# First feed-forward layer on tokens sorted by expert in DRAM, with the whole first attention ahead of it

## What is computed

```
x = x + _L0_xattn_ref(_layernorm(x), ctx, ...)        # one head, 32 keys per sequence
x = x + _L0_ffn_ref(_layernorm(x), ...)               # 8 experts, each token uses ONE (argmax of the gates)
x = x + _L1_xattn_ref(_layernorm(x), ctx, ctx, ...)   # 16 heads, 32 keys
x = x + _L1_ffn_ref(_layernorm(x), ...)               # 16 experts, top 4 per token, and a shared expert
```

## Time and profile before

| | |
|---|---|
| time, median of 3 runs | 404.8 us (399.02 and 426.97 the others) |
| the profiled execution | span 400.2 us from the first to the last instruction; that page gives no time beside it |
| TensorE, VectorE, ScalarE, GpSimd busy | 355.2, 252.4, 189.4, 165.3 us |
| chain that ended last | TensorE 62%, VectorE 22%, issue 9% |
| DMA | 8.14 MB, mean 20 GB/s |

### The profile page before, as it was taken

One profiled execution on the slowest core, in us unless ns is written; L12 is line 12 of the kernel. 1 busy time (PEld: TensorE's weight loads), 2 busy tenths in 40 slices (PEclk: granted clock), 3 DMA queues, 4 the chain that ended last, 5 costly groups with the idle time before them and its releaser, 6 DMA issues.

```text
span 400.2 us, 5681 instructions
## 1 busy us (share of the span) xinstructions
PE 355.2 (89%) x1871; PEld 276.1 (69%) x1875; DVE 252.4 (63%) x608; ACT 189.4 (47%) x316; POOL 165.3 (41%) x161
## 2 busy tenths in 40 slices
PE   0885999999999999999889967797849999999995
PEld 0673778877787788777466756574528878878883
DVE  4445526644564454863799999979974665665652
ACT  1525524662546364545455533474424445444452
POOL 5539302100210151432385631736743555555553
PEclk9988699999999999999999998999978999999998
DMA  7604000000000000000000000000000000000000
GB/s 264 247 1 162 7 2 1 2 0 2 1 1 2 2 0 2 1 2 1 0 2 1 2 0 0 2 1 1 0 0 2 27 2 0 26 0 0 26 0 26
DMA packets 2408, 8.14 MB, mean 20 GB/s; under 512 B 432, under 2 KB 544, under 8 KB 2000
## 3 DMA queue, kind: packets, MB, share of 16 engines
q1 hardware_dynamic: 1984, 6.49, 4.4%
q10 hardware_dynamic: 400, 1.34, 1.0%
HBM read 6.78 MB, written 1.05 MB: 20 GB/s over the span
## 4 chain that ended last, share of the span: by engine, by line
PE 62%; DVE 22%; issue 9%; ACT 2%; DMA 2%; POOL 1%; POOLq 0%; another core or an unknown queue 0%; SPq 0%; ACTq 0%; DVEq 0%
PE bank L1112 58%; DVE xn L808 3%; DVE sc L944 3%; DVE mx L937 2%; PE bank L1124 2%; DMA pack_a<-in_pack_a 2%; DVE act L1073 1%; DVE z L949 1%; DVE st L797 1%; PE bank L1299 1%; DVE bqrep L878 1%; DVE rz L953 1%; PE bank L1163 1%; DVE route L972 1%; POOL an L738 1%
## 5 line engine op out<-in xcount | busy, mean ns | idle before, releaser
L759 POOL TENSOR_TENSOR w1l<-hm,w1h 128x512 fp32r<-128x512 f32 x48 | 62.2, 1298 | 41.8 <-ACT w1h L604 41.6
L913 DVE TENSOR_TENSOR hm<-act,bank 128x512 f32<-128x512 f32 x64 | 43.3, 685 | 52.3 <-ACT act L520 51.6
L1112 PEld LDWEIGHTS bank<-w,hm 128*128 128x128 f32 x512 | 65.6, 195 | 10.1 <-issue 5.1
L1112 PE MATMUL bank<-w,hm 128*128 128x128 f32 x512 | 71.8, 286 | 0.1
L520 ACT ACTIVATE act<-bank,pack_b 128x512 f32<-128x512 f32 x64 | 43.4, 687 | 56.6 <-PE bank L1112 55.9
L1073 DVE TENSOR_TENSOR act<-act,bank 128x512 f32<-128x512 f32 x48 | 33.0, 687 | 38.9 <-ACT act L619 38.7
L619 ACT ACTIVATE act<-bank 128x512 f32<-128x512 f32 x48 | 28.7, 598 | 51.8 <-PE bank L1112 51.5
L663 POOL TENSOR_SCALAR ve<-mv 128x4 f32<-128x4 f32 x16 | 3.7, 228 | 113.0 <-DVE mv L801 109.0
L1112 PE MATMUL bank<-xTh,gu1h 128*128 (+3 forms) x104 | 43.5, 418 | 2.4 <-DVE act L1073 2.4
L1112 PE MATMUL bank<-xTh,gu1l 128*128 (+3 forms) x104 | 41.8, 402 | 0.0
L1112 PE MATMUL bank<-xTl,gu1h 128*128 (+3 forms) x104 | 41.6, 400 | 0.0
(11 more groups left out here) (198 smaller groups left out, 671.5 us busy)
## 6 DMA issues: line engine op xcount, KB each, us to landing
wf<-in_gu SPq DMA_DIRECT2D x1, 1632.0 KB, 7.2
x<-in_x SPq DMA_DIRECT2D x4, 256.0 KB, 9.3
wf<-in_w ACTq DMA_DIRECT2D x1, 1024.0 KB, 6.6
w<-in_w SPq DMA_DIRECT2D x1, 1024.0 KB, 11.4
out_x<-x SPq DMA_DIRECT2D x4, 256.0 KB, 2.0
w<-in_w SPq DMA_DIRECT2D x1, 768.0 KB, 12.7
pack_a<-in_pack_a SPq DMA_DIRECT2D x1, 455.0 KB, 6.0
pack_b<-in_pack_b SPq DMA_DIRECT2D x1, 360.0 KB, 8.4
```

What stands on the lines that cost most here:

```text
L759: nc.gpsimd.tensor_tensor(hml_slot(r)[0:m], hm_slot(r)[0:m], hmh_slot(r)[0:m].bitcast(F32), ALU.subtract).then_inc(s.hml_ready, 1)
L913: nc.vector.tensor_tensor(hm[:, r % 4, :], act[:, r % 4, :], bank[2 + r // 2 % 2][:, :], ALU.mult).then_inc(s.hm_ready, 1)
L1112: return nc.tensor.matmul(dst, lhsT, rhs, start=start, stop=stop, skip_group_check=True)
```

## The change

The first feed-forward layer is computed for one expert per token. The items and `AFTER` are gone, and so is `experts0`. In their place, in order of time:

1. **First attention ahead.** `STEPS0` has 14 steps; in step s chunk c does stage k = s - 2c, of `STAGES0` = 8 (0 statistics; 1 norm, transposes, scores; 2 shift and exp; 3 softmax and output; 4 residual and statistics; 5 norm and logits; 6 one-hot; 7 slot). `normalise` is on ScalarE now, as `x * rstd + shift_of`; `rstd_of` has two small instructions more on GpSimd.
2. **Slots and tables.** Matmuls with a triangle and with ones count the tokens of the same expert ahead of each token; `slot0` is expert x REGION + rank. GpSimd writes each normalised tile of 128 rows to its slots in DRAM (`scatter`, 16 indirect DMAs, in stage 7 of each chunk). About 12 VectorE instructions on one partition (`over0` to `tile_r`) work out, for each of T0 = 16 + 8 - 1 = 23 row tiles, its expert and its first row. SyncE reads them into registers, and writes zero rows behind the last token of each expert (9 DMAs).
3. **23 row tiles.** SyncE loads, per tile, the expert's weights `wb` (128x642, 321 KB) and the rows `xs` (128x128, 64 KB) into SLOTS0 = 4 buffers. TensorE transposes the rows, multiplies by W1, and one tile later by W2, all plain FP32; VectorE copies the transpose and adds b2, ScalarE does Gelu; GpSimd stores each result to DRAM (23 DMAs).
4. **Back.** When all are stored, GpSimd fetches each tile of 128 tokens with an indirect DMA (`fetch`, 16; 8 ahead of the second attention, 8 in its steps), and VectorE adds `score * y` to `x` (`combine`).
5. **Second attention.** As before, but all four chunks' query norms stand in or just ahead of it. The rounding of its neighbour's weights is ahead of or among the row tiles: high halves on ScalarE, low halves on VectorE.

`experts1` is unchanged except that `normalise` is on ScalarE.

```diff
-AFTER = {XT: 0, SCORES: 1, EXP0: 2, SOFTMAX: 3, ATTN_T: 5, OUT: 6, NORM2: 7, XT2: 9, LOGITS: 10, EXP0G: 11, GATES: 12,
-         GATES_T: 14, BIAS2: 15, STATS: 14, NORM: 15}
+STAGES0, LAG0 = 8, 2
+STEPS0 = [[(s - LAG0 * c, c) for c in range(B) if 0 <= s - LAG0 * c < STAGES0] for s in range(STAGES0 + LAG0 * (B - 1))]
...
+            for t in range(0, T0, SLOTS0):
...
+                for u in own:
+                    if u >= SLOTS0:
+                        sp.wait_ge(s.y0_ready, u - SLOTS0 + 1)
+                    load_weights(u, experts[u - t])
+                    if u == 0:
+                        sp.wait_ge(s.scattered, 16 * NT)
+                        sp.wait_ge(s.padded, 16 * (E0 + 1))
+                    load_tokens(u, first[u - t])
...
+            for t in range(T0):
+                pool.wait_ge(s.y0_ready, t + 1)
+                pool.dma_start(ys_dram[t * P:(t + 1) * P, :], ys[:, t % SLOTS0, :]).then_inc(s.kept_y[t % SLOTS0], 16)
+            pool.wait_ge(s.home_ready, 1)
+            for i in range(SLOTS0):
+                pool.wait_ge(s.kept_y[i], 16 * len(range(i, T0, SLOTS0)))
+            for t in range(2 * TPB):
+                fetch(t)
+            rstd_of(2, 0)
...
+            for t in range(T0 + 2):
+                if t < T0:
+                    pe.wait_ge(s.ld_xs[t % SLOTS0], rounds0(t))
...
+                    nc.tensor.transpose(bank[t % 2][:, 0:P], xs[:, t % SLOTS0, :], ident).then_inc(s.xs_mm, 1)
+                if 1 <= t <= T0:
+                    u = t - 1
+                    pe.wait_ge(s.ld_wb[u % SLOTS0], rounds0(u))
+                    pe.wait_ge(s.xsT_ready, u + 1)
...
+                        last = mm(bank[2 + u % 2][:, k * P:(k + 1) * P], w0_1[:, u % SLOTS0, k, :], xsT[:, u % 2, :])
...
+                if t >= 2:
+                    u = t - 2
+                    pe.wait_ge(s.h0_ready, u + 1)
...
+                        last = mm(bank[4 + u % 2][:, 0:C], hT0[:, u % 2, k, :], w0_2[:, u % SLOTS0, k, :],
+                                  start=(k == 0), stop=(k == HID0 - 1))
```

More of the change, by code:

```diff
@@ L14 @@
 F32R = mybir.dt.float32r
+I32 = mybir.dt.int32
 BF16 = mybir.dt.bfloat16
@@ new lines, in _, with round_gu, round_w2 @@
+            keys_values(3)
+            def round_gu(n):
+                w, q = divmod(n, 4)
+                width = (R1 * P + I1) // 4
+                nc.scalar.copy(gu1h[:, w, q * width:(q + 1) * width], gu1f[:, w, q * width:(q + 1) * width]).then_inc(s.guh_ready, 1)
+            def round_w2(n):
+                src, rows, own = w2_piece(n)
+                nc.scalar.copy(w2h[rows, own, :], src).then_inc(s.w2h_ready, 1)
+            act_e.wait_ge(s.ld_gu, 16)
+            for n in range(PIECES):
+                round_gu(n)
@@ L739, in _ @@
                                             ALU.mult).then_inc(s.an1_ready, 1)
-                if i == LN3:
-                    rstd_of(2, B - 1)
+                for b in ahead(i, FETCH3):
+                    rstd_of(2, b)
+                if i + 2 * TPB < NT:
+                    fetch(i + 2 * TPB)
                 for b in starts(i, ADD):
@@ new lines, in _ @@
+            v.wait_ge(s.ld_b, 16)
+            step(nc.vector.tensor_scalar(bo16[:, :], bo1, 1.0 / H1, None, ALU.mult))
+            v.wait_ge(s.kv_ready, 4)
+            for b in range(B):
+                block_diagonal(vT1, Vblk, b, s.vblk_ready)
+            v.wait_ge(s.move_mm, 1)
+            step(nc.vector.tensor_tensor(rk0[:, :, :, :].rearrange("p b j e -> p (b j) e"), rows_of(bank[0][:, 0:E0], NT), oh16[:, :, :], ALU.mult))
+            step(nc.vector.tensor_reduce(z0[:, :, :].rearrange("p b j -> p (b j)"), rk0[:, :, :, :].rearrange("p b j e -> p (b j) e"), AX, ALU.add))
@@ L934, in maxima, with combine @@
+            def combine(b):
+                v.wait_ge(s.fetched[b], 16 * TPB)
+                for t in range(b * TPB, (b + 1) * TPB):
+                    last = nc.vector.scalar_tensor_tensor(x[:, t, :], xn2[:, t, :], score0[:, t:t + 1], x[:, t, :], ALU.mult, ALU.add)
+                last.then_inc(s.x2_ready, 1)
+                v.wait_ge(s.x2_ready, b + 1)
             def maxima(i):
                 v.wait_ge(s.s1_mm, i + 1)
-                scores = score_bank(i)[:, :].rearrange("p (h k) -> p h k", h=H1)
+                scores = bank[i % 2][:, :].rearrange("p (h k) -> p h k", h=H1)
@@ L1046, in _ @@
                     inverse(i - 1)
-                if i == LN3:
-                    statistics(2, B - 1)
-                if i == NORM3:
-                    normalise(2, B - 1)
+                for b in ahead(i, FETCH3):
+                    combine(b)
+                    statistics(2, b)
                 for b in starts(i, ADD):
@@ new lines, in _ @@
+            pe.wait_ge(s.slot_ready, B - 1)
+            for t in range(NT):
+                last = mm(bank[6][0:1, 2 * P:2 * P + E0], onesb[:, 0:1], oh16[:, t, :], start=(t == 0), stop=(t == NT - 1))
+            last.then_inc(s.total_mm, 1)
+            pe.wait_ge(s.ld_b, 16)
+            pe.wait_ge(s.table_ready, 2)
+            keys_values(2, attn1_w[:, 0, :])
+            keys_values(3, attn1_w[:, 2, :])
+            pe.wait_ge(s.move_ready, 1)
+            mm(bank[0][:, 0:E0], onesb[0:1, :], move0[:, :]).then_inc(s.move_mm, 1)
@@ L1451 @@
         "order8": rows(np.arange(E0, 0, -1, dtype=np.float32)),
+        "tri": np.triu(np.ones((P, P), np.float32), 1),
+        "base": rows(np.tile(np.arange(E0, dtype=np.float32) * REGION, TPB)),
     }
```

1035 lines of the change are left out of this document (526 added, 509 removed).

## The result

The changed kernel takes 421.17 us (median of 5 runs, 418.44 to 424.81), against 401.14 for the kernel before in the same comparison. The ratio is 1.046, 95% interval [1.038, 1.055]: slower. The forecast was 382 us and faster, with a range to 412. Some executions of every kernel are slower by a per cent or two at a lower granted clock: ratios leave them out and medians do not, a8_holdrev had too few others for such a ratio, and f1b_depthlead's profile is of a slow one, so its stages are left out.

What follows compares the result with a forecast made beforehand. It took four consecutive stages as the bound, TensorE ending last in the removed first feed-forward layer. Terms 68 + 14 + 68 + 21 + 54 + 153 gave 378 us, plus 4.6 for the median: 382, range 354 to 412.

Steps and rivals of the forecast that it cites:

- A: All of the first attention, from the start to the last slot: 68 us, bounds 51 to 90.
- each chunk holds it ... 10.5 us in all: First attention: TensorE, working in order, is held by each chunk's transposes, waited-for copies and products for 10.5 us.
- short turns: Rival, chance 0.22: TensorE stays at its upper clock and loads land faster; row tiles 11 us, first attention 8 shorter; 363 us.
- 6.75 + 3.75 per pair: First attention: two steps of one chunk's chain last 6.75 us, plus 3.75 lost where three chunks share TensorE.
- B: From the last slot to the first row tile (zero writes, tables, register rows, first loads): 14 us, bounds 10 to 30.
- The rival with SyncE as the bound: Rival, chance 0.12: register rows at 0.48 us each make SyncE's batch change overtake two row-tile turns; 424 us, slower.
- C: The 23 row tiles: two tiles per 6.3 us turn of load and compute, register rows hidden; 68 us, bounds 49 to 99.
- D: From the last row-tile result to the second attention's first score: store, fetches, norm, query; 21 us, bounds 15 to 26.
- E: The second attention: 54 us, bounds 51 to 60.
- A step of VectorE takes 1.98 us and bounds it: Second attention: VectorE's steps of 1.98 us set the pace, with norms moved to ScalarE and statistics and additions added.
- F: The second feed-forward layer, its loop the same code: 153 us, bounds 149 to 156.
- no gain that can be seen: Rival, chance 0.16: row-tile turns of 7.5 us from slower landings, and indirect DMAs at 1.8 us; 402 us.

Runs made afterwards that it cites:

- a8_holdrev: The change with chunk c+1's output ahead of chunk c's second norm in odd first-attention steps, wide products and extra matmuls in its gaps; 421.1 us.
- f1b_depthlead: The change with row-tile transposes behind both products (three tiles per turn) and second-attention norms started further ahead (leads 7, 6, 4, 2); 403.9 us.
- a5_hold2: The change with first-attention scores and logits 128 columns wide and the larger set of extra, overwritten bf16 matmuls in TensorE's gaps there; 406.4 us.
- c1_depth3: The change with TensorE's transpose of row tile t behind the products of tiles t-1 and t-2, VectorE's copy likewise behind the addition; 409.1 us.
- e3_hold: The change with second-attention leads 7, 6, 4, 2, and extra overwritten matmuls in TensorE's waits from the last result to the fifth tile; 409.9 us.
- e5_expfirst: The change with second-attention leads 7, 6, 4, 2, and ScalarE's exponentials of tiles 0 and 1 ahead of chunk 1's copy and query; 409.8 us.
- e4_fetch16: The change with second-attention leads 7, 6, 4, 2, and all 16 fetches ahead of the loop; 411.4 us.
- a2_wide: The change with scores and logits of the first attention computed 128 columns wide, as in the kernel before; 419.7 us.
- e2b_leadwarm: The change with second-attention leads 7, 6, 4, 2, and 60 extra overwritten matmuls ahead of its first transposes; 411.8 us.

## Why the prediction was wrong, by its own steps

**A, forecast 68, measured 84.7: the step that failed is "each chunk holds it ... 10.5 us in all".** Its terms, as they stand there, add to 9.5 and not 10.5; by them A would have been about 65, further off still. It read TensorE's durations from the earlier trace rows, most of them from 18.85 us on, where the level was the upper one. The same work at the lower level is 14.0 us of the 16.6 of a pair: transposes 1.1 twice, products 1.9 twice, 1.0, the output 5.8, score offsets and ranks 1.2. The forecast had the sign of a low clock in the earlier trace rows and took the upper level for A all the same: its rival of short turns says "I have half counted it" and would take 8 us off A at the upper level, but the terms of A already stand at that level for the most part. For chunks 1 to 3 one had been the dense layer's wide matmuls, which stood between all these small ones at a clock of 0.98 and are gone. Chunk 0's rows were at the upper level even before the first of them (the second row below), so the dense layer is not all of it, and what brought the level up there is not shown:

```profile
19.27 0.48 PE L1112 MATMUL bank<-V,aT 32*128 32x128 f32 x2
...
32.12 0.47 PE L1112 MATMUL bank<-xTh,w1h 128*128 128x512 f32 x1 [1.54 <-ACT V L510]
```

With the upper level held for most of the stage, a5_hold2 is 12.4 us shorter; that is what the level costs in A. The other part is that the hand-over was priced as a sum with overlap (6.75 + 3.75 per pair) instead of followed as a ring; with the level held it was 12.9 per pair against 10.5, read from the chain and not from a run that removed the ring.

**B, 14 against 15.5: right.** The register rows, taken as 0.12 us each with nothing to price them, took 0.30 for the first of a table (up to 0.83 in the change), then by turns 0.15 and 0.02, with 0.04 between: 18 of them last 2.7 us in c1_depth3 (123.37 to 126.07), 0.15 each. Two parts were too small, the zero writes (5.4 us against 3.8) and the landing (3.1 against 2.3), and the 14 taken stood above the 13 of the sum. The rival with SyncE as the bound is false, since it needed 0.34 per row; but the rows are not hidden, as C assumed: at a change of batch they stand in the chain.

```profile
123.37 0.30 SPq L518
123.70 0.15 SPq L518
```

The Trainium skill, page "Runtime: NRT & Kernel Launch", section "Instruction fetch mechanics", gives about 200 ns per register loaded; here eight table entries in 2.7 us are 0.34 each, with the second row of each entry and the longer first row of each table in it.

**C, 68 against 70.3: right in size and mechanism**, shown by c1_depth3. The landing was 3.0 to 3.1 against 3.3, and the register rows in the chain make up for that. By the fit of the Trainium skill's page "DMA: Bandwidth & Descriptors" ("Anatomy of one DMA — SWDGE (gpsimd) path") the 64 KB of `xs` would land in an estimated 2.15 us and the 321 KB of `wb` in 2.75; here they land alike, in 3.0 and 3.1. The page gives its fit for DMAs that GpSimd issues, and SyncE issues these two; GpSimd's own 64 KB stores landed in 3.1 us as well.

**D, 21 against 23.9: right in mechanism.** 2.6 of the 2.9 are the clock: e3_hold has 21.3. ScalarE's norm, too, took 1.65 us where 1.1 was put. A fetch costs 0.95 us and 0.30 to the next, 1.25, where 1.2 was taken.

**E, 54 against 73.7: the step that failed is "A step of VectorE takes 1.98 us and bounds it".** The work on VectorE was forecast well (busy 53.72), and so was what it exchanges: norms away, combines and statistics in. But the norms that left stood in a part of the loop that got no faster by it (all behind 207.88 us; from the seventh maxima to the sixteenth VectorE was busy 29.5 of 29.8 us before, 24.4 of 30.4 in e5_expfirst), and what came in stands ahead of a chain of 13 us that has four steps of lead. The prediction named the risk only for the fetches, and `combine` waits for none of them inside the loop. The leads gave 7.3 us and ScalarE's order 2.9 more. Of the 9.1 left over the kernel before, 8.4 lie in the first six tiles: 4.6 are added work on VectorE and 3.8 its waits, of which the clock (1.0, e3_hold) and the fetches (about 1, e4_fetch16) may be parts; the rest stays open.

**F, 153 against 152.7: right.** The 4.6 us added at the end for the median were not there: the execution with the span of 420.8 took 422.6 us, and the median of the runs is 421.2.

The rivals: "no gain that can be seen" named slow landings and dear indirect DMAs, and neither came. "Short turns" needed the upper level. The one slower case, SyncE's, is not the one that came true. None was the case that did, the lower level and the hand-overs in A and E, for which the earlier trace rows and the bounds of A (up to 90) had the signs. The measured 84.7 lies inside those bounds; the error was to take 68 from within them. Two signs named for being wrong did come, the last slot after 80 us and E over 60, the second without the waiting `combine` that it was named for.

## What to carry to other kernels

A dense layer that is taken away can also have been the filler between small steps of other stages: reckon what is left at TensorE's lower level too, and as the longest closed ring of hand-overs, read from the order of each engine's stream, not as work plus some overlap. Where work is moved to stand just ahead of its use, count the whole chain from its first instruction to that use and compare it with the lead in steps. And a ring of buffers is as deep as the order of the engine that uses it allows.

## What the runs showed of the hardware

- The granted clock of a stretch can mislead where no change of it is recorded yet. In the first 84.7 us of the change the column reads 1.00, while four transposes take 1.12 us, as at the lower level; the durations of equal matmuls are the better sign.
- Small FP32 matmuls back to back did not always bring the upper level: in the change the output products of a chunk with the transposes and scores that followed kept TensorE busy from 33.91 to 43.88 us with gaps of only 0.25, and stayed at 0.79 per pair. But FP32 work without any bf16 matmul of 512 columns did bring it elsewhere: the same pairs took 0.48 in the kernel before (19.27 us) and in a2_wide (17.60 us, behind products of 512 and 128 columns from 10.08 on where the change has 128 and 32), and there went back to 0.79 at 19.41. What decides is not shown. With extra bf16 matmuls of 512 columns in the gaps they took 0.48 in a5_hold2.
- Narrow products save nothing at the lower level: eight FP32 products took 1.92 us with 32 columns (the change, 41.63 us) and 1.84 with 128 (a2_wide, 41.31 us). At the upper level eight with 128 columns took 1.05 (a5_hold2, 35.50 us).
- After a wait of 0.95 us TensorE was still at the upper level (e3_hold), after one of 3.96 us it was at the lower (e2b_leadwarm). The wait alone does not tell: after 3.25 us the transposes still took 0.66 in a5_hold2 (66.73 us), and the next eight products 2.08.
- Extra work on TensorE made the kernel faster: a5_hold2 takes 406.4 us with 1462 recorded matmul rows on TensorE, the change 421.2 with 1360, and TensorE is busy for about the same time in both, 306.4 and 305.1 us.
